# The decay matrix N of a chunked delta rule, made by four VectorE operations straight from the exponential

## The reference

```python
def step(S, inp):
    qt, kt, vt, gt, bt = inp
    S = S * jnp.exp(gt)[:, None, None]
    kv = jnp.einsum('hk,hkv->hv', kt, S)
    delta = (vt - kv) * bt[:, None]
    S = S + kt[:, :, None] * delta[:, None, :]
    o = jnp.einsum('hk,hkv->hv', qt, S)
    return (S, o)
```

## Time and profile before

| What | us |
|---|---|
| median of 3 runs | 2921.76 |
| lowest of the runs | 2921.57 |
| the profiled execution, its own time | 2925.89 |
| its span in the profile | 2924.2 |
| PE busy | 2763.0 |
| DVE busy | 2184.5 |
| ACT busy | 1801.5 |
| POOL busy | 1616.3 |

### The profile page before, as it was taken

The page is one execution under the profiler, slowest core; times in us unless marked ns, Lnnn a source line. Parts: engine busy times, 40 slices in busy tenths (PEclk is TensorE's granted clock), DMA queues, the critical chain, the costliest instruction groups (busy, mean ns, idle before and its releaser), DMA issues. The chain is left out here.

```text
span 2924.2 us, 75635 instructions
## 1 busy us (share of the span) xinstructions
PE 2763.0 (94%) x24303; PEld 1893.4 (65%) x24303; DVE 2184.5 (75%) x4677; ACT 1801.5 (62%) x6310; POOL 1616.3 (55%) x3737
## 2 busy tenths in 40 slices
PE   5999579999999999999999999999999999869998
PEld 4556356666676666666766776666676667645555
DVE  3433468888888888888888888888888887637776
ACT  3322557777777777777777777777777776323332
POOL 1000367777777776677777767777776777310000
PEclk9999889999999999999999999999999999969999
DMA  3000121222222222222221222222222222110000
GB/s 91 0 1 0 29 50 36 53 44 53 43 49 40 47 44 47 50 46 54 37 51 36 53 44 54 43 48 40 47 45 51 47 47 42 23 44 0 8 8 15
DMA packets 485567, 113.69 MB, mean 39 GB/s; under 512 B 423296, under 2 KB 484336, under 8 KB 485168
## 3 DMA queue, kind: packets, MB, share of 16 engines
q1 hardware_dynamic: 485168, 108.76, 18.4%
HBM read 80.63 MB, written 28.06 MB: 37 GB/s over the span
## 5 line engine op out<-in xcount | busy, mean ns | idle before, releaser
L1221 DVE SCALAR_TENSOR_TENSOR S<-S,gs,bank 128x128 f32<-128x128 f32 x1024 | 286.8, 342 | 212.1 <-PE bank L781 207.6
L548 POOL TENSOR_TENSOR Tb<-Tb,btmp 64x14 f32<-64x14 f32 (+6 forms) x896 | 325.1, 363 | 70.3
L544 POOL TENSOR_TENSOR btmp<-Bk,Tb 64x14 f32<-64x14 f32 (+6 forms) x896 | 325.9, 364 | 65.3
L933 ACT ACTIVATE sq_kq<-bank 128x128 bf16<-128x128 f32 x512 | 134.3, 277 | 287.8 <-PE bank L689 287.8
L460 POOL TENSOR_SCALAR ty<-ty 128x4 f32<-128x4 f32 x128 | 109.6, 856 | 357.9 <-issue 319.4
L1252 DVE SCALAR_TENSOR_TENSOR conv<-raw,cv,conv 128x512 f32<-128x512 f32 x384 | 295.7, 783 | 13.8 <-ACT conv L1006 8.8
L1252 DVE SCALAR_TENSOR_TENSOR conv<-raw,ckq,conv 128x512 f32<-128x512 f32 x384 | 293.8, 779 | 13.7 <-ACT conv L1006 9.0
L738 PE MATMUL bank<-xnT,wkq 128*128 128x512 f32 x512 | 256.9, 626 | 10.6 <-POOL mkX L429 10.6
L1004 ACT ACTIVATE raw<-bank 128x512 f32<-128x512 f32 x256 | 154.0, 602 | 177.1 <-PE bank L738 173.4
L824 PE MATMUL bank<-wout_h,gT 128*128 128x256 f32 x1024 | 258.1, 395 | 0.0
L738 PE MATMUL bank<-xnT,wv 128*128 128x512 f32 x512 | 255.8, 623 | 0.0
(11 more groups left out here) (354 smaller groups left out, 6714.1 us busy)
## 6 DMA issues: line engine op xcount, KB each, us to landing
rowb<-decay_rows SPq DMA_DIRECT2D x256, 64.0 KB, 4.0
blk_n<-N SPq DMA_DIRECT2D x256, 64.0 KB, 2.5
Tp<-blk_t SPq DMA_DIRECT2D x128, 128.0 KB, 3.0
Wp<-blk_w SPq DMA_DIRECT2D x128, 128.0 KB, 3.1
wkq<-in_L_attn_W_qkvz_dram SPq DMA_DIRECT2D x32, 128.0 KB, 2.2
wv<-in_L_attn_W_qkvz_dram SPq DMA_DIRECT2D x16, 256.0 KB, 4.2
Bk<-blk_n SPq DMA_DIRECT2D x64, 64.0 KB, 2.6
blk_t<-Tb SPq DMA_DIRECT2D x64, 64.0 KB, 2.5
```

Source lines behind the costliest of these rows:

```text
L544: pool.tensor_tensor(tmp, Bk[:, j, j + 1:].unsqueeze(2).broadcast_to([64, 15 - j, j]), Tb[:, j, 0:j].unsqueeze(1).broadcast_to([64, 15 - j ...
L548: pool.tensor_tensor(Tb[:, j + 1:, 0:j], Tb[:, j + 1:, 0:j], tmp, ALU.subtract).then_inc(row_rdy, 1)
L1221: i = dve.scalar_tensor_tensor(out=S[:, 2 * b + v, :], in0=S[:, 2 * b + v, :], scalar=gs[t.c][:, kind, 2 * h + v:2 * h + v + 1], in1=pKU[b ...
```

## The change

POOL's scaled copy ETn (`scaled`) goes, with its buffer and its semaphore. DVE's `strict` no longer multiplies ETn with the Gram matrix in one tensor_tensor over all four units; it makes N from ET with four scalar_tensor_tensor operations, one for each unit, each (ET x CC of the unit, a scalar per partition) x Gram matrix. DVE waits for the exponential and for CC itself, in place of ETn. The exponential of the next step waits for N in place of ETn.

```diff
-        ETn = sb("ETn", [P, U, H])
...
-                def scaled(s):
-
-                    t = s.back(S_F)
-                    if not t.live:
-                        return
-                    pool.wait_ge(exp_rdy, t.done())
-                    pool.wait_ge(der_rdy, t.done())
-                    wait(pool, N_rdy, t.done(1))
-                    pool.tensor_tensor(ETn[:], ET[:], ty[t.c][:, CC, :].unsqueeze(2).broadcast_to([P, U, H]),
-                                       ALU.mult).then_inc(ETn_rdy, 1)
-
...
                     derive(s)
-                    scaled(s)
                     causal(s)
...
                     act.wait_ge(rel_rdy, t.done())
-                    wait(act, ETn_rdy, t.done(1))
+                    wait(act, N_rdy, t.done(1))
                     wait(act, ET_rdy, t.done(1))
...
-                    dve.wait_ge(ETn_rdy, t.done())
+                    dve.wait_ge(exp_rdy, t.done())
+                    dve.wait_ge(der_rdy, t.done())
                     dve.wait_ge(gram_mm, t.done())
                     wait(dve, x16_mm, t.done(RING))
                     wait(dve, n_out, t.at(32, 32 - 32 * RING))
-                    split = lambda a: a.rearrange("p (s v) n -> p s v n", s=2)
-                    dve.tensor_tensor(split(N[t.c % RING][:]), split(ETn[:]),
-                                      pGram[:, :, 0, :].unsqueeze(2).broadcast_to([P, 2, 2, H]), ALU.mult).then_inc(N_rdy, 1)
+                    for u in range(U):
+                        i = dve.scalar_tensor_tensor(out=N[t.c % RING][:, u, :], in0=ET[:, u, :],
+                                                     scalar=ty[t.c][:, CC, u:u + 1], in1=pGram[:, u // 2, 0, :],
+                                                     op0=ALU.mult, op1=ALU.mult)
+                    i.then_inc(N_rdy, 1)
```

More of the change, by code:

```diff
@@ L219, in delta_rule @@
                             "o1_rdy", "o2_rdy", "o3_rdy", "sc_rdy"))
-        lower_rdy, ETn_rdy, le4_rdy = ev("lower_rdy"), ev("ETn_rdy"), ev("le4_rdy")
+        lower_rdy, le4_rdy = ev("lower_rdy"), ev("le4_rdy")
         rowb_in, rel_rdy = [ev(f"rowb{r}_in") for r in range(2)], ev("rel_rdy")
```

## The result

The changed kernel takes 2930.39 us (median), the kernel before 2922.51 us in the same comparison: a ratio of 1.0028, with a 95% interval of 1.002 to 1.0036. So the change costs 0.3%, some 8 us. Forecast were 23 us. The sign and the range hold; the size is a third of it. One of the 16 runs of the kernel before was a slow one of 5439.89 us, and the ratio leaves it out. The profiled execution took 2930.17 us, with a span of 2928.4.

What follows compares the result with a forecast made beforehand. PE was taken as the bound. A 31 us stall at the solve, nothing for ACT and 8 us saved by POOL's relief gave 23 us on 2921.76, rounded to 2945 us, 0.8% slower; range 2913 to 2981.

Steps and rivals of the forecast that it cites:

- The sign and the range: Whole kernel: slower, 2945 us or 0.8%, with a range of 2913 to 2981 us.
- PE as the bound: Steady loop: PE busy 1685.46 of 1700 us, so a late result costs its lateness in full in each slot.
- Nothing that only unloads another engine can save more than the 15 us that PE is idle there: Window 600 to 2300 us: PE's idle time, 15 us, caps any saving from unloading another engine.
- The cost of the four operations: DVE making N: four at 0.193 us each, 0.77 us, 0.44 us more than the one operation.
- The lower bound: DVE making N: pointer scalar adds no fixed cost, 0.13 us each, 0.52 for four, 0.19 us more.
- full durations: Rival on DVE: each small operation starts after the last ends, 1.10 us for four, 2985 us; chance 0.16 including a floor.
- The stall: PE at the solve: R 0.44 us later less 0.19 margin, 0.25 us in 123 slots, 31 us, bounds 0 to 64.
- ScalarE's exponential: ACT: exponential waits for N, 1.4 us late, hidden behind the late solve; cost nothing, bounds 0 to 14 us.
- never below nothing, as ACT only waits longer: ACT's new wait for N: it can cost 0 to 14 us but cannot save time.
- GpSimd's relief: POOL's chain through blk_t to Tp: removing its operation shortens PE's waits for Tp, saving 8 us, bounds 0 and 12.
- POOL is almost 0.6 us earlier: POOL at the rows of the block inverse: without the scaled copy it arrives almost 0.6 us earlier.
- not slower: Rival: small operations cost 0.19 us more, margin takes it up, only POOL's earlier rows count, -8 us, 2914; chance 0.14.

Runs made afterwards that it cites:

- e6: Kernel before with GpSimd's scaled copy out, N by one tensor_tensor from ET without CC, and R's second half ahead of the second tap: 2897.13 us, ratio 0.9903.
- e3: Kernel before with N's one tensor_tensor cut into four tensor_tensor 128x64 from ETn, no pointer scalar: 2945.6 us, ratio 1.0082.
- e5: Changed kernel with two buffers for ET, so the exponential no longer waits for N of the same slot: 2937.09 us, ratio 1.0046 against the kernel before.
- e4: Changed kernel with the second half of R made ahead of DVE's second tap: 2910.65 us, ratio 0.9969 against the kernel before.
- e7: Changed kernel with two buffers for ET and R's second half ahead of the second tap: 2909.31 us, ratio 0.9947 against the kernel before.
- e11: Changed kernel with two ET buffers and R ahead of the second tap, but the exponential waiting for N of the same slot: 2913.96 us, 0.9972 against kernel before.
- e10: Kernel before with one wait added, the exponential also waiting for N of the step before: 2925.38 us, ratio 1.0004.
- e1: Kernel before with GpSimd's scaled copy out, N still one tensor_tensor straight from ET, CC left out, exponential waiting for N: 2909.21 us, ratio 0.9957.
- e12: Kernel before with two swaps only, R ahead of the second tap and the exponential behind the second copying out: 2926.5 us, ratio 0.9996.

## Why the prediction was right or wrong

- PE as the bound, and a late result costing its lateness in full: right. The slot grew by 0.28 us, the solve's 0.23 and 0.05 behind it.
- "Nothing that only unloads another engine can save more than the 15 us that PE is idle there": wrong. PE's busy time rose from 1685.46 to 1693.77 us in the slower kernel, so it also counts time lost. By the starts of its groups 27.5 us were lost, and e6, in which PE has the same work and one operation of GpSimd is out, is 25 us faster.
- The cost of the four operations: right. 0.77 us was forecast from the S updates, 0.77 measured, so 0.44 more. The lower bound, 0.13 us each, is the price of a tensor_tensor of that size (e3), and "full durations" fell.
- The stall: 0.25 us a slot was forecast, 0.28 measured, 31 against 33.8 us. What was short is the handover: a late solve also hands over 0.05 us later to the next group.
- ScalarE's exponential: its cost is right, the bound is not. 1.4 us late was forecast, it stands idle for 1.43 us, hidden behind the late solve (e5), at 0.10 us a slot where that cover is gone (e4), forecast 0.11. But "never below nothing, as ACT only waits longer" failed: without the wait the changed kernel is 5 us slower (e5), and with R first x16 loses 8.1 us without the wait and 1.3 with it (e7, e11).
- GpSimd's relief: this is the step that failed, the term "I take 8 us, bounds 0 and 12". In its place the irregular losses fell by 27.5 - 2.2 = 25.3 us, with the solve's irregular loss counted in, and 33.8 - 25.3 = 8.5 us are left of the forecast 23. Its direction and its chain (GpSimd, blk_t, Tp, PE) were right. Four parts of its size failed. First, I took the waits' rows at their word: 9.9 us in 1700 us, 12.5 us for the loop, while the starts of PE's groups show 16.8 at x16. Second, I counted only the wait itself; each such slot lost another 0.2 to 0.4 us at the second solve, 6.4 us in all, since DVE's tap then ran into GpSimd's operation. Third, I did not count the waits for wz, 4.3 us. Fourth, not all of it is GpSimd's: ScalarE's new wait brought the slow landings down from 28 to 5 of 57 (e5 against the changed kernel), and x16 from 7.5 to 2.2 us. Without GpSimd's operation gone the same wait gave nothing (e10).
- "POOL is almost 0.6 us earlier": in the even slots blk_t was issued 12.18 us after PE's first transposes of the slot (median), and is now issued after 10.93. That is 1.25 us, more than the operation's 0.61. GpSimd's product of Bk with the triangle, which took 1.29 us (median) beside DVE's tap, now takes 0.84; the remaining 0.2 us are not traced.
- The rival "not slower", 2914 us, had its gain from the relief right in kind. With N still one operation, the relief and ScalarE's wait together give 12 us (e1), and 25 once R stands ahead of the tap (e6).
- The prediction reads the Trainium skill's section "The DRAIN you can't avoid" (page "VectorE: DVE Perf Modes") too narrowly: the section goes on to say that a next operation that is not held starts earlier. The starts 0.26 us apart at 0.34 us of duration agree with that.

Of the collision, the Trainium skill, page "SBUF — State Buffer", section "SBUF: two separate sides", says that a DVE operation with two SBUF inputs and a GpSimd operation that reads SBUF exclude one another, the later one waiting for the whole of the earlier. The rows agree: the tap reads two SBUF tensors and takes 1.16 or 1.36 us beside L521 or L533. In all three timelines above it ends 0.54 or 0.55 us after GpSimd's operation (1509.16 and 1509.71; 1384.55 and 1385.10; 1532.20 and 1532.74 us), wherever it began, as if its 0.74 us started 0.19 us before the recorded end of the other. N, with one input from PSUM, is not stretched by the same operation at 1519.20 in the changed kernel. This rule should have been weighed ahead of the prediction; by the timeline of the kernel before, L533 and the second tap were neighbours.

## What to carry to other kernels

When an engine off the critical path is relieved, look for all waits of the bound engine whose chain runs through it, and price them from the starts of its instructions, since the rows of waits name only the idle part. When work moves onto an engine with slack, place it behind the results that the bound engine needs next: here two swaps in two hand-written orders turned a loss of 8 us into a gain of 26, while the same swaps without the change gained nothing (e12). A new wait on an engine off the critical path is not free of effect either: it moves what that engine and its fetches meet.

## What the runs showed of the hardware that was not expected

- A 16 KB instruction packet beside a write of 64 KB in small packets goes with a landing of 4.3 us in place of 2.5. All 167 writes with such a packet 0.3 to 1.87 us behind their issue were slow, 29 of 143 with one from there to 2.5 us, and none of the 470 writes with no instruction packet from 0.5 us ahead to 2.5 us behind. An 8 KB packet alone, at 0.8 to 1.5 us, goes with 2.8 to 3.3 us, in 22 of 22 (all 14 runs; the times are to the issue of Tp). A single wait on ScalarE moved the slow landings from 23 to 2 of 57 (e7, e11).
- DVE's tap of 0.74 us takes 1.16 to 1.36 us when a GpSimd operation on SBUF tensors has started just before it. In the kernel before, the GpSimd operation was often the later one and took 1.29 us, and the tap took 0.75.
- A scalar_tensor_tensor of 128x64 with a pointer scalar costs 0.19 us from start to start, a tensor_tensor of the same size 0.13 (changed kernel, e3).
